# A graph attention edge pass that steps on one TensorE semaphore, with GpSimd's gathers behind it

## The chip, the cores and the metric

One core of a Trainium2 chip. The metric is the device time of one execution in microseconds, from the chip's own counters; the profile is a separate execution of the same program, traced instruction by instruction. A time of before is the median of three runs.

## What is computed

One block over 6250 nodes with 256 channels and 200000 edges sorted by their destination. The part that the change touches is the attention over edges:

```python
h = (x @ W.T).reshape(n, H, D)            # H = 8 heads of D = 32
h_src, h_dst = h[src], h[dst]
enc = jax.nn.relu(edge_attr @ edge_W.T + edge_b).reshape(-1, H, D)
alpha = (jnp.einsum('ehd,hd->eh', h_src, a_src) + jnp.einsum('ehd,hd->eh', h_dst, a_dst)
         + jnp.sum(enc * h_dst, axis=-1))
alpha = jnp.where(alpha >= 0, alpha, 0.2 * alpha)
amax = jax.ops.segment_max(alpha, dst, num_segments=n)
ex = jnp.exp(alpha - amax[dst])
denom = jax.ops.segment_sum(ex, dst, num_segments=n)
out = jax.ops.segment_sum(h_src * (ex / denom[dst])[..., None], dst, num_segments=n)
```

Around it stand a layer norm, a linear attention layer with its feed forward part, and a feed forward part with eight experts of which each node takes one. The change leaves those alone.

## The kernel before

The kernel runs its stages one after the other: node features and linear attention first, then the edge pass, then routing and experts. The edge pass works through 440 items (`ITEMS`). An item is 512 edges (`SE`) against one tile of 125 nodes. Four items (`G`) make a group, and there are 110 groups (`NG`). The code of every engine is written out for every step `k`, so the order on an engine is the order of the program text, and each engine works on several items at different lags in one step.

For item `n`, in order:

- GpSimd `gather(n)` (L506 to L515): four indirect DMAs, each bringing 128 rows of `h_tab` (272 floats a row) into one of 16 slots (`RING`). It waits for the item's earlier transfers, for `msg_ready` (the message of item n-16 is made, so the slot is free) and for `m_used`.
- ScalarE `load_item` (L735 to L738) brings destinations and edge attributes, three DMAs, into one of four buffers.
- TensorE `e_enc` (L1031) encodes the attributes in two matmuls, ScalarE `e_relu` (L753) takes them through the relu, VectorE `e_onehot` (L1452) compares the destinations with the tile's nodes, TensorE `e_dst` (L1041) spreads the nodes' features in six matmuls.
- VectorE `e_prod` (L1461) multiplies, in two halves, and TensorE `e_sum` (L1062, 16 small matmuls; L1065 on every fourth item) sums by head into bank 7.
- For each group a chain on VectorE, TensorE and ScalarE finds the running maxima across edges and the exponentials: `g_x`, `g_leaky`, `g_fmax` (L1479), `g_smax`, `g_up`, `g_ends`, `g_chain`, `g_fin`, `g_down`, `g_carry`, `g_fmax2` (L1510), `g_smax2` (L1514 and L1515, which signals `x_dif`), `g_exp`, `g_turn`, `g_keep`, `g_delta`, `g_fac`, `g_scale` (L1533).
- ScalarE `keep_asrc` (L760) copies eight columns of the gathered rows one step after the item's encoding, so it waits for the gather; `m_dt` and `m_oneh` (L764 to L775) make another one-hot matrix.
- VectorE `m_msg` (L1541) weights the gathered rows, TensorE `m_sum` (L1100, 8 matmul instructions in the trace) sums them by node, VectorE `m_acc` (L1550) adds the sum to the accumulator.

`LM` is the lag of `m_msg` behind the item's first step: 11 before.

SyncE runs a loop over groups (L440 to L445): `load_idx(g)` waits until the items of group g-2 are gathered and issues four DMAs (L412), then `load_links(g-2)` waits for `x_dif` of the group two before that one and issues 24 small DMAs (16 at L420 into `pen`, 8 at L423 into `link`). `g_fmax` of a group waits for all 24 (`links_in`).

Before, each kind of TensorE work signals a semaphore of its own: `enc_mm`, `d_ready`, `r_ready`, `ends_up`, `ends_down`, `ex_turned`, `m_used`. ScalarE, VectorE and GpSimd wait for these one by one. In the bank 7 code, what TensorE writes and the others read shares one bank, which `bank7_read` guards.

Of the kernel before, what the change touches and what calls it, by code (L numbers as in the profile page):

```python
# [20 lines left out]
ALU = mybir.AluOpType  # L21
ACT = mybir.ActivationFunctionType
X = mybir.AxisListType.X
ds = bass.ds
# [3 lines left out]
P = 125  # L28
# [5 lines left out]
SE = 512  # L34
# [15 lines left out]
CLEARS = 10  # L50
# [4 lines left out]
LM = 11  # L55
# [51 lines left out]
def build_program(nc, io):  # L107
    stack = ExitStack()
    with stack:
# [42 lines left out]
        def slot(n):  # L152
# [103 lines left out]
        fin = sb("fin", [33, 128], at=mem_e)  # L256
        carry = sb("carry", [128, 2], at=mem_e)
        xs, exr = small[0], small[3]
# [71 lines left out]
        item_in, oneh_t_ready, d_ready, enc_ready = sems("item_in", EB // 2), sem("oneh_t_ready"), sem("d_ready"), sem("enc_ready")  # L330
        enc_mm, prod_ready, r_ready, zeroed = sem("enc_mm"), sem("prod_ready"), sem("r_ready"), sem("zeroed")

        links_in = sems("links_in")
        x_kept, x_local, ends_up, ends_read, links_made, ends_down, carry_read, x_dif, x_exp, ex_turned, ex_kept = (
            sem("x_kept"), sem("x_local"), sem("ends_up"), sem("ends_read"), sem("links_made"), sem("ends_down"), sem("carry_read"), sem("x_dif"), sem("x_exp"), sem("ex_turned"), sem("ex_kept"))
        dl_ready, fac_ready, acc_scaled = sem("dl_ready"), sem("fac_ready"), sem("acc_scaled")
        dt_ready, msg_ready, oneh_ready, dist_ready, acc_added, m_used = sem("dt_ready"), sem("msg_ready"), sem("oneh_ready"), sem("dist_ready"), sem("acc_added"), sem("m_used")
# [47 lines left out]
        def _(sp):  # L385
# [59 lines left out]
            sp.wait_ge(m_used, ITEMS)  # L445
# [28 lines left out]
        def _(pool):  # L474
# [29 lines left out]
            def gather(n):  # L504
# [6 lines left out]
                wait(pool, m_used, n - RING)  # L511
# [21 lines left out]
            clear(fin[:, :], 0.0)  # L533
# [9 lines left out]
            pool.wait_ge(m_used, ITEMS)  # L543
# [48 lines left out]
        def _(act):  # L592
# [142 lines left out]
            def load_item(b, s):  # L735
                act.dma_start(dstb[b][:, :], dst16[ds(s * SE, SE)].partition_broadcast(P)).then_inc(item_in[b // 2], 16)
                for a in range(KC):
                    act.dma_start(att[b][32 * a:32 * a + 24, :], attrx[:, ds(s * SE, SE)]).then_inc(item_in[b // 2], 16)  # L738
# [10 lines left out]
            def e_relu(n):  # L749
                act.wait_ge(enc_mm, n + 1)  # L750
# [5 lines left out]
            def keep_asrc(n):  # L756
                i = n % G
                act.wait_ge(gathered[n % NGS], 64 * (n // NGS) + 64)
                wait(act, r_ready, n - i - G)
# [6 lines left out]
            def m_oneh(n):  # L766
# [7 lines left out]
                wait(act, m_used, n - NM + 1)  # L774
                act.activation(oneh[n % NM][:, :, :], dist[q][:, :, :], ACT.Relu, bias=1.0, scale=-1.0).then_inc(oneh_ready, 1)  # L775

            def g_x(g):
                act.wait_ge(r_ready, G * g + G)
                wait(act, x_dif, g)
                act.activation(xs[:, :], bank[7][:, 0:128], ACT.Copy).then_inc(x_kept, 1)  # L780
# [5 lines left out]
            def g_keep(g):  # L786
                act.wait_ge(ex_turned, g + 1)
# [5 lines left out]
            def g_fac(g):  # L793
                act.wait_ge(ends_down, g + 2)
# [18 lines left out]
            for k in range(ITEMS + LM + 2):  # L813
# [5 lines left out]
                if (g := group_at(k, 5)) is not None:  # L819
                    g_x(g)  # L820
                if (g := group_at(k, 9)) is not None:
                    g_exp(g)
                if (g := group_at(k, 10)) is not None:
                    g_keep(g)
                if 0 < k < ITEMS - EB + 1:
                    b = k % EB
                    act.wait_ge(d_ready, k)
# [4 lines left out]
                if k % G == 0 and 8 <= k < ITEMS + 8:  # L832
                    s_dt, t_dt = item_regs(act, 0, k - 8), item_regs(act, 1, k - 8)
                if 0 <= k - 8 < ITEMS:
# [3 lines left out]
                if (g := group_at(k, 12)) is not None:  # L838
                    g_fac(g)

            act.wait_ge(m_used, ITEMS)
# [44 lines left out]
        def _(pe):  # L886
# [139 lines left out]
            def e_enc(n):  # L1026
                b = n % EB
                pe.wait_ge(item_in[b // 2], 96 * (n // EB) + 96)
# [785 lines left out]
```

## Time and profile before

| what | value |
|---|---|
| median of the runs | 4996.56 us (4992.17 to 4997.22) |
| the profiled execution | 5021.78 us |
| its span, first to last instruction | 5019.9 us |
| granted TensorE clock, mean | 0.864 |
| TensorE matmuls busy | 3767.7 us, 75% |
| VectorE busy | 2605.4 us, 52% |
| ScalarE busy | 2110.6 us, 42% |
| GpSimd busy | 2107.5 us, 42% |
| edge pass, first `m_acc` to last | 984.1 to 4232.6 us, 440 items |

Busy time is what an engine's own instructions took; waiting and DMA issue are not in it. In a group of rows, "idle before" is the time that the engine stood still just before these instructions, and the name behind the arrow is what the trace sees end that wait. "remote" or "another core or an unknown queue" is said where the trace finds nothing that ended at that time.

### The profile page before, as it was taken

Reading aid. Unit: us, or ns where it says so; the run is one execution under the profiler, and the core shown is the slowest. Engines: PE = TensorE matmul, PEld = TensorE weight load, DVE = VectorE, ACT = ScalarE, POOL = GpSimd, SP = SyncE. Lnnn points to the kernel's source line nnn. Section 1 sums busy time; section 2 is a strip of 40 time slices with the busy share of each in tenths; the row PEclk is TensorE's granted clock in tenths of the full one; section 3 lists DMA queues with packets and bytes.
Section 4 is the critical chain, followed back from the end, with each engine's and each line's share of the span. In section 5 each row is a group of like instructions: output and inputs, shape, how many; then the busy total and the mean of one; then the engine's idle time right before and its main releaser. Section 6 shows DMA issues by size and latency. Waiting matters only on the chain.

```text
span 5019.9 us, 89713 instructions
## 1 busy us (share of the span) xinstructions
PE 3767.7 (75%) x22054; PEld 2525.2 (50%) x22055; DVE 2605.4 (52%) x6056; ACT 2110.6 (42%) x5703; POOL 2107.5 (42%) x2172
## 2 busy tenths in 40 slices
PE   4788998477777677677777777777777775972999
PEld 3357887244444444444444444444444443862888
DVE  5557555455555555555555655555655555440121
ACT  3212332244444444454444545444454444442332
POOL 4120000455555555555555555555555551015111
PEclk8889999788888888888888888888888888986999
DMA  4610111344433344343433444334444443002110
GB/s 153 218 60 18 32 33 37 89 100 102 106 99 101 99 104 105 100 105 103 105 104 103 110 105 110 103 102 104 106 111 107 104 110 119 30 22 58 36 37 29
DMA packets 352311, 449.36 MB, mean 90 GB/s; under 512 B 170970, under 2 KB 275163, under 8 KB 350456
## 3 DMA queue, kind: packets, MB, share of 16 engines
q0 software_dynamic: 95568, 267.78, 20.6%
q10 hardware_dynamic: 108050, 122.83, 7.9%
q1 hardware_dynamic: 148231, 53.53, 4.4%
q8 instruction: 174, 2.85, 0.2%
q14 instruction: 288, 2.36, 0.1%
HBM read 389.57 MB, written 55.13 MB: 89 GB/s over the span
## 4 chain that ended last, share of the span: by engine, by line
PE 48%; another core or an unknown queue 16%; issue 13%; DVE 11%; ACT 4%; ACTq 4%; DMA 3%; POOL 1%; DVEq 1%; SPq 0%; POOLq 0%
PE bank L1100 9%; PE bank L1041 8%; PE bank L1184 4%; PE bank L1196 4%; PE bank L1144 4%; PE bank L1006 3%; PE bank L1015 3%; PE bank L1062 3%; DVE prod L1461 3%; PE bank L1031 2%; ACT dist L771 2%; DVE msg L1541 2%; PE bank L919 1%; PE bank L1065 1%
## 5 line engine op out<-in xcount | busy, mean ns | idle before, releaser
L515 POOL DMA_INDIRECT al<-h_tab,idx x976 | 1022.7, 1048 | 794.9 <-issue 298.5
L515 POOL DMA_INDIRECT gbuf<-h_tab,idx x784 | 840.5, 1072 | 808.8 <-issue 383.8
L753 ACT ACTIVATE enc<-bank,eb 128x512 f32<-128x512 f32 x880 | 555.9, 682 | 1468.2 <-remote 1262.5
L1062 PE MATMUL bank<-prod,hsel 128*32 128x128 f32 x7040 | 325.6, 309 | 763.0 <-issue 505.1
L1041 PE MATMUL bank<-oneh_t,hbt 125*128 125x512 bf16 x2640 | 842.3, 463 | 46.8 <-issue 39.4
L1062 PEld LDWEIGHTS bank<-prod,hsel 128*32 128x32 f32 x7040 | 192.1, 119 | 934.3 <-issue 634.2
L1461 DVE SCALAR_TENSOR_TENSOR prod<-enc,adst,bank 128x512 f32<-128x512 f32 x880 | 629.1, 736 | 37.9 <-remote 32.4
L1100 PE MATMUL bank<-msg,oneh 128*125 128x264 f32 x2352 | 628.5, 413 | 26.9 <-DVE r L1550 18.0
L1100 PEld LDWEIGHTS bank<-msg,oneh 128*125 128x125 f32 x2352 | 488.1, 208 | 173.0 <-issue 61.1
L771 ACT ACTIVATE dist<-iota_n,dtile 128x125 f32<-128x125 f32 x1760 | 550.9, 384 | 0.2
L1041 PEld LDWEIGHTS bank<-oneh_t,hbt 125*128 x2640 | 257.5, 111 | 493.0 <-issue 365.6
L1550 DVE TENSOR_TENSOR r<-r,bank 125x264 f32 x440 | 188.2, 428 | 559.4 <-remote 263.5
L1100 PE MATMUL bank<-al,oneh 128*125 128x264 f32 x1168 | 314.0, 413 | 10.9 <-DVE r L1550 7.2
L1100 PEld LDWEIGHTS bank<-al,oneh 128*125 128x125 f32 x1168 | 241.5, 208 | 90.1 <-issue 34.3
L775 ACT ACTIVATE oneh<-dist 128x500 f32<-128x500 f32 x440 | 272.7, 620 | 14.1 <-PE bank L1100 0.2
L1031 PE MATMUL bank<-att,ew_bf 24*128 24x512 bf16 x880 | 206.1, 453 | 48.9 <-DMA att<-attrx 28.3
L524 POOL MEMSET al<- 128x2 f32 (+1 forms) x3 | 0.3, 113 | 535.7 <-DMA accd<-al 535.6
L880 ACT ACTIVATE al<-bank,b1f 128x256 f32<-128x256 f32 x224 | 106.2, 474 | 270.6 <-PE bank L1184 270.6
L1541 DVE TENSOR_TENSOR msg<-al 128x1056 f32<-128x1056 f32 x163 | 203.8, 1250 | 0.1
L1184 PE MATMUL bank<-al 128*128 128x256 f32 x896 | 200.8, 383 | 0.7 <-ACT al L874 0.7
L1015 PE MATMUL bank<-r 128*125 128x256 f32 x800 | 200.2, 379 | 0.0
L1006 PE MATMUL bank<-r 128*128 128x250 f32 x800 | 199.2, 378 | 0.0
(255 smaller groups left out, 5405.9 us busy)
## 6 DMA issues: line engine op xcount, KB each, us to landing
dstb<-dst ACTq DMA_DIRECT2D x440, 125.0 KB
al<-pen_d SPq DMA_DIRECT2D x1760, 4.0 KB
att<-attrx ACTq DMA_DIRECT2D x880, 24.0 KB
al<-h_tab,idx POOLq DMA_INDIRECT x976
link<-links SPq DMA_DIRECT2D x880, 0.2 KB
gbuf<-h_tab,idx POOLq DMA_INDIRECT x784
attrx<-al ACTq DMA_DIRECT2D x8, 1176.0 KB, 12.3
hsplit<-hb POOLq DMA_DIRECT2D x25, 375.0 KB, 5.4
```

What stands on the lines that cost most here:

```text
L515: pool.indirect_dma_start(slot(n)[:, c, :], None, h_tab, bass.IndirectOffsetOnAxis(ap=idx[g % 2][:, k:k + 1], axis=0)).then_inc(gathered[n ...
L753: m = act.activation(enc[n % 2][:, k, :], bank[k][:, :], ACT.Relu, bias=eb[:, k:k + 1])
L771: m = act.activation(dist[q][:, c, :], iota_n[:, :], ACT.Abs, bias=dtile[n % NDT][:, c:c + 1], scale=-1.0)
L1006: m = pe.matmul(bank[FB3[j % 4]][:, 0:W2T], w1m[:, k, j * 128:(j + 1) * 128], ynT[:, k, :], start=(k == 0), stop=(k == KC - 1))
L1015: m = pe.matmul(bank[3 + u][0:P, 0:C], f1[:, j, u * P:(u + 1) * P], w2m[:, j, :], start=(j == 0), stop=(j == JF - 1))
L1031: m = pe.matmul(bank[k][:, :], ew_bf[32 * k:32 * k + 24, k * 128:(k + 1) * 128], att[b][32 * k:32 * k + 24, :], start=True, stop=True)
L1041: m = pe.matmul(bank[2 + 2 * q + k][:, :], hbt[:, ds(t & (HT - 1), 1), a, k * 128:(k + 1) * 128].rearrange("p t c -> p (t c)"), oneh_t[q][ ...
L1062: m = pe.matmul(bank[7][32 * c:32 * c + 32, 0:128], hsel[:, i, :], prod[n % 2][:, k, c * 128:(c + 1) * 128], start=(i == 0 and k == 0), st ...
L1100: m = pe.matmul(bank[6][0:P, 0:HO], oneh[n % NM][:, c, :], msg[n % NM][:, c, :], start=(c == 0), stop=(c == 3))
L1184: m = pe.matmul(bank[FB[j % 4]][:, 0:256], w1f[:, k, j * 128:(j + 1) * 128], xdT[:, k, :], start=(k == 0), stop=(k == KC - 1))
L1461: m = v.scalar_tensor_tensor(prod[q][:, k, :], enc[q][:, k, :], adst[:, k:k + 1], bank[2 + 2 * q + k][:, :], ALU.add, ALU.mult)
L1541: v.tensor_tensor(msg[n % NM][:, :, :].rearrange("p c (h e) -> p c h e", h=H), slot(n)[:, :, 8:HR].rearrange("p c (h e) -> p c h e", h=H), ...
```

## The change

Each TensorE step now ends with one signal, `stepped`, on the last matmul of `e_enc(k + 1)` (in the last steps on `m_sum`). All seven semaphores above are gone. VectorE and ScalarE wait for `stepped` once, at the top of a step, and what a step takes from TensorE is what TensorE finished in the step before. For this the lags grow: `LM` is 14, the group's chain takes lags 6, 9, 11 and 13 instead of 6, 7, 8 and 11 on VectorE, and some buffers are doubled (`fin`, `xs`, `smax2`). TensorE's step now runs spread, message sum, sum by head, the group's small matmuls, next encoding. GpSimd's gather of item n waits for `stepped` to reach n, which is the end of TensorE's step n-2. Each item buffer has a semaphore of its own (`item_in[b]`) instead of one for two. SyncE's loop keeps its text; only its wait after the loop names `stepped`.

```diff
-LM = 11
+LM = 14
+STEPS = ITEMS + LM + 2
@@ GpSimd, gather(n)
                 wait(pool, msg_ready, n - RING + 1)
-                wait(pool, m_used, n - RING)
+                wait(pool, stepped, min(n, STEPS) if n >= RING else 0)
@@ ScalarE
             def e_relu(n):
-                act.wait_ge(enc_mm, n + 1)
                 wait(act, prod_ready, n - 1)
...
-            for k in range(ITEMS + LM + 2):
+            for k in range(STEPS):
+                act.wait_ge(stepped, k + 1)
+                if (g := group_at(k, 6)) is not None:
+                    g_x(g)
...
-                    m_dt(k - 8, s_dt[k % G], t_dt[k % G])
-                if 0 <= k - 10 < ITEMS:
-                    m_oneh(k - 10)
...
+                    m_dt(k - 12, s_dt[k % G], t_dt[k % G])
+                if 0 <= k - 13 < ITEMS:
+                    m_oneh(k - 13)
+                if (g := group_at(k, 11)) is not None:
+                    g_exp(g)
@@ TensorE
+            e_enc(0).then_inc(stepped, 1)
+            for k in range(ITEMS + LM + 1):
                 if k % EB == 0 and k < ITEMS:
                     t = item_regs(pe, 1, k, EB)
+                if k < ITEMS:
+                    e_dst(k, t[k % EB])
+                if 0 <= k - LM - 1 and k + 1 < ITEMS:
+                    m_sum(k - LM - 1)
                 bank7_read(k)
                 if 0 <= k - 2 < ITEMS:
                     e_sum(k - 2)
...
+                if k + 1 < ITEMS:
+                    e_enc(k + 1).then_inc(stepped, 1)
+                else:
+                    m_sum(k - LM - 1).then_inc(stepped, 1)
@@ VectorE
-                g1, g2, g3, g4 = (group_at(k, lag) for lag in (6, 7, 8, LM))
+                g1, g2, g3, g4 = (group_at(k, lag) for lag in (6, 9, 11, 13))
+                v.wait_ge(stepped, k + 1)
```

TensorE, one step in the middle of the edge pass, before (the encoding and the spread of one item, then the message sum; `msg`, `oneh`, `prod` as above, `ident` is the identity):

```order
L1062 MATMUL bank<-prod,hsel 32x128 [waits prod_ready,x_kept]
L1062 MATMUL bank<-prod,hsel 32x128 x7
L1092 MATMUL bank<-ident,al 1x8 [waits x_exp]
L1093 MATMUL bank<-ident,al 128x128
L1031 MATMUL bank<-att,ew_bf 128x512 [waits enc_ready,item_in1]
...
L1037 REGISTER_ALU [waits oneh_t_ready]
...
L1041 REGISTER_ALU [waits prod_ready,node_in]
...
L1041 MATMUL bank<-oneh_t,hbt 128x512
...
L1100 MATMUL bank<-al,oneh 125x264 [waits acc_added,oneh_ready,msg_ready]
```

The same of the changed kernel:

```order
L1035 REGISTER_ALU [waits oneh_t_ready]
...
L1039 REGISTER_ALU [waits prod_ready,node_in]
...
L1039 MATMUL bank<-oneh_t,hbt 128x512
...
L1098 MATMUL bank<-msg,oneh 125x264 [waits acc_added,oneh_ready,msg_ready]
...
L1061 MATMUL bank<-prod,hsel 32x128 [waits prod_ready,x_kept]
L1061 MATMUL bank<-prod,hsel 32x128 x7
L1079 MATMUL bank<-ident,fin 128x2 [waits links_made]
L1085 MATMUL bank<-dl,oneh 125x8 [waits oneh_ready,dl_ready]
L1029 MATMUL bank<-att,ew_bf 128x512 [waits enc_ready,item_in3]
```

The message sum and its wait for the accumulator moved ahead of the sum by head, and the encoding moved to the end, where it carries the step's signal.

VectorE, the step in which a group's first scan (`g_fmax`) stands, before:

```order
L1550 ISA [waits acc_added,m_used]
L1550 TENSOR_TENSOR r<-r,bank 125x264
L1474 SCALAR_TENSOR_TENSOR al<-al 128x128 [waits ex_turned,x_kept]
L1461 SCALAR_TENSOR_TENSOR prod<-enc,adst,bank 128x512 [waits r_ready,enc_ready,d_ready]
L1479 SCALAR_TENSOR_TENSOR al<-al 128x128 [waits own_step,links_in1]
L1461 SCALAR_TENSOR_TENSOR prod<-enc,adst,bank 128x512
L1483 SCALAR_TENSOR_TENSOR al<-al 128x128 [waits own_step]
...
L1452 TENSOR_SCALAR oneh_t<-dstb,nid 125x512
L1541 TENSOR_TENSOR al<-al 128x1056 [waits m_used,gathered5,ex_kept]
```

and of the changed kernel:

```order
L1548 ISA [waits acc_added,stepped]
L1548 TENSOR_TENSOR r<-r,bank 125x264
L1462 SCALAR_TENSOR_TENSOR prod<-enc,adst,bank 128x512 [waits enc_ready]
L1474 SCALAR_TENSOR_TENSOR al<-al 128x128 [waits x_kept]
L1462 SCALAR_TENSOR_TENSOR prod<-enc,adst,bank 128x512
L1479 SCALAR_TENSOR_TENSOR al<-al 128x128 [waits own_step,links_in1]
...
L1455 TENSOR_SCALAR oneh_t<-dstb,nid 125x512
L1483 SCALAR_TENSOR_TENSOR al<-al 128x128 [waits own_step]
L1540 TENSOR_TENSOR al<-gbuf,al 128x1056 [waits gathered2,ex_kept]
```

All waits for TensorE but the first are gone; the scan stands behind both products instead of between them, with the wait for the links still on it.

## Rows read from the trace of the kernel before

**Rows 1.** Windows: busy time of each engine in the middle of the edge pass
```profile
core 0: us, PE busy (x) PEld busy (x) DVE busy (x) ACT busy (x) POOL busy (x), PEclk, DMA share, GB/s
1200.00:4000.00 2800.00, 2057.82 (x13187) 1215.80 (x13187) 1596.52 (x3253) 1352.63 (x3805) 1577.34 (x1485) 0.84 0.40 104
```

**Rows 2.** Windows, of line L1550 (`m_acc`, one an item) alone
```profile
core 0: us, DVE busy (x), PEclk, DMA share, GB/s
1200.00:4000.00 2800.00, 158.71 (x371) 0.84 0.40 104
```

**Rows 3.** Waits, 1500 to 3500 us: who waited for whom, us in total, times, longest
```profile
ACT enc L753 <- remote: 768.0, 151, 9.1
...
DVE r L1550 <- remote: 179.1, 50, 6.1
DVE al L1474 <- remote: 162.2, 25, 8.3
...
DVE carry L1506 <- remote: 105.2, 22, 7.0
```

**Rows 4.** Timeline, 2500 to 2520 us, TensorE's work and who saw it (start, us)
```profile
2501.14 0.39 PE L1031 MATMUL bank<-att,ew_bf 24*128 24x512 bf16 x2
...
2502.77 1.95 PE L1100 MATMUL bank<-msg,oneh 128*125 128x264 f32 x8
...
2506.21 0.69 ACT L753 ACTIVATE enc<-bank,eb 128x512 f32<-128x512 f32 x1 [6.16 <-remote]
...
2507.43 0.43 DVE L1550 TENSOR_TENSOR r<-r,bank 125x264 f32 x1 [3.49 <-remote]
...
2514.17 0.29 DVE L1474 SCALAR_TENSOR_TENSOR al<-al 128x128 f32<-128x128 f32 x1 [6.32 <-remote]
...
2518.25 0.61 PE L1031 MATMUL bank<-att,ew_bf 24*128 24x512 bf16 x2
...
2518.90 0.69 ACT L753 ACTIVATE enc<-bank,eb 128x512 f32<-128x512 f32 x1 [0.65 <-PE bank L1031]
```

**Rows 5.** Timeline of GpSimd, 2491 to 2520 us
```profile
2500.72 0.94 POOL L515 DMA_INDIRECT al<-h_tab,idx  x1 [0.30 <-issue]
...
2505.07 0.95 POOL L515 DMA_INDIRECT al<-h_tab,idx  x1 [0.30 <-issue]
2508.16 0.95 POOL L515 DMA_INDIRECT al<-h_tab,idx  x1 [2.15 <-remote]
...
2511.92 0.95 POOL L515 DMA_INDIRECT al<-h_tab,idx  x1 [0.30 <-issue]
2518.62 0.94 POOL L515 DMA_INDIRECT al<-h_tab,idx  x1 [5.75 <-DVE al L1541]
```

**Rows 6.** Groups by line, 1200 to 4000 us: busy us, mean ns, idle before
```profile
L515 POOL DMA_INDIRECT al<-h_tab,idx x837 | 884.9, 1057 | 688.9 <-issue 256.9 <-DVE msg L1541 177.7 <-PE bank L1100 106.3
L1041 PE MATMUL bank<-oneh_t,hbt 125*128 125x512 bf16 x2232 | 712.2, 463 | 35.1 <-issue 34.4
L515 POOL DMA_INDIRECT gbuf<-h_tab,idx x648 | 693.6, 1070 | 534.0 <-issue 185.4 <-PE bank L1100 119.0 <-DVE msg L1541 103.2
L1461 DVE SCALAR_TENSOR_TENSOR prod<-enc,adst,bank 128x512 f32<-128x512 f32 x744 | 532.0, 736 | 0.3
...
L771 ACT ACTIVATE dist<-iota_n,dtile 128x125 f32<-128x125 f32 x1484 | 464.5, 384 | 0.2
...
L775 ACT ACTIVATE oneh<-dist 128x500 f32<-128x500 f32 x371 | 229.9, 620 | 11.8
```

**Rows 7.** Timeline of TensorE, 4220 to 4240 us: the last steps, without gathers
```profile
4227.69 2.02 PE L1100 MATMUL bank<-msg,oneh 128*125 128x264 f32 x8 [0.50 <-DVE r L1550]
4230.43 2.02 PE L1100 MATMUL bank<-msg,oneh 128*125 128x264 f32 x8 [0.72 <-DVE r L1550]
```

**Rows 8.** Timeline of SyncE: first and last issues of three groups' links
```profile
2593.49 1.73 SPq L420 DMA_DIRECT2D al<-pen_d  x4
...
2608.71 1.21 SPq L423 DMA_DIRECT2D link<-links  x2
...
2528.51 1.38 SPq L420 DMA_DIRECT2D al<-pen_d  x4
...
2545.38 1.17 SPq L423 DMA_DIRECT2D link<-links  x2
...
1373.31 4.37 SPq L420 DMA_DIRECT2D al<-pen_d  x4
...
1393.18 1.21 SPq L423 DMA_DIRECT2D link<-links  x2
```

**Rows 9.** The page's DMA issues: KB each, median us from issue to landing
```profile
hsplit<-hb POOLq DMA_DIRECT2D x25, 375.0 KB, 5.4
```

**Rows 10.** Timeline of VectorE: the scan of the first of these groups, its step
```profile
2630.46 0.43 DVE L1550 TENSOR_TENSOR r<-r,bank 125x264 f32 x1 [4.17 <-PE bank L1100]
...
2631.90 0.42 DVE L1479 TENSOR_TENSOR_SCAN al<-al 128x128 f32<-128x128 f32 x1
...
2633.45 1.25 DVE L1541 TENSOR_TENSOR msg<-al 128x1056 f32<-128x1056 f32 x1
```

**Rows 11.** Timeline of VectorE: the step that signals `x_dif` (L1515)
```profile
1369.89 0.43 DVE L1550 TENSOR_TENSOR r<-r,bank 125x264 f32 x1 [0.18 <-issue]
...
1372.84 0.29 DVE L1515 TENSOR_TENSOR al<-al 128x128 f32<-128x128 f32 x1
```

More of the change, by code:

```diff
@@ L49 @@
 NM = 3
-CLEARS = 10
+CLEARS = 11
 NDT = 4
@@ L255, in build_program @@
         tot = sb("tot", [33, H, 17], at=mem_e)
-        fin = sb("fin", [33, 128], at=mem_e)
+        fin = [sb(f"fin{q}", [33, 128], at=mem_e) for q in range(2)]
         carry = sb("carry", [128, 2], at=mem_e)
-        xs, exr = small[0], small[3]
+        xs, exr = [small[0], al[:, spare + 1280:spare + 1408]], small[3]
+        smax2 = al[:, spare + 1152:spare + 1280]
         fmax, smax = al[:, spare + 128:spare + 256], al[:, spare + 288:spare + 416]
@@ L532, in _ @@
             clear(tot[:, :, 16:17], -BIG)
-            clear(fin[:, :], 0.0)
+            for q in range(2):
+                clear(fin[q][:, :], 0.0)
             clear(edge[:, :, 0:1], -BIG)
@@ L773, in m_oneh @@
                 act.wait_ge(dist_ready, n + 1)
[L774 removed]
                 act.activation(oneh[n % NM][:, :, :], dist[q][:, :, :], ACT.Relu, bias=1.0, scale=-1.0).then_inc(oneh_ready, 1)
             def g_x(g):
[L778 to L780 removed]
+                wait(act, x_dif, g - 1)
+                act.activation(xs[g % 2], bank[7][:, 0:128], ACT.Copy).then_inc(x_kept, 1)
             def g_exp(g):
@@ L1040, in e_dst, with readings @@
                     for a in range(3):
[L1041 to L1042 removed]
+                        pe.matmul(bank[2 + 2 * q + k][:, :], hbt[:, ds(t & (HT - 1), 1), a, k * 128:(k + 1) * 128].rearrange("p t c -> p (t c)"), oneh_t[q][:, :], start=(a == 0), stop=(a == 2))
             def bank7_read(k):
[L1046 to L1047 removed]
+                def readings(lag):
+                    return min((k - lag) // G, NG - 1) + 1 if k >= lag else 0
+                if k % G == 2:
+                    wait(pe, x_kept, readings(6))
                 if k % G == 1:
[L1049 to L1052 removed]
+                    wait(pe, ends_read, readings(9))
+                    wait(pe, ex_kept, readings(13))
                 if k % G == 3:
[L1054 removed]
+                    wait(pe, carry_read, readings(11))
+                    wait(pe, fac_ready, readings(15))
             def e_sum(n):
@@ L1112, in _ @@
                     e_sum(k - 2)
-                elif k % G == 2:
+                elif k % G == 2 and k < ITEMS + LM:
                     new_sums()
@@ L1556, in _ @@
             e_onehot(0, item_regs(v, 1, 0)[0])
-            for k in range(ITEMS + LM + 3):
+            for k in range(STEPS):
                 if k % G == 0:
```

162 lines of the change are left out of this document (69 added, 93 removed).

## The prediction

> **What bounds the kernel now.** The table by windows comes first. In the middle of the edge pass no engine is full: TensorE is busy 2058 of 2800 us, GpSimd 1577, VectorE 1597, ScalarE 1353 [rows 1]. Line L1550 runs once an item, 371 times in 2800 us [rows 2], so a step takes 2800 / 371 = 7.55 us, and 440 of them make about two thirds of the span. What a step is made of must be read from the waits. The largest are put down to nothing that the trace knows: ScalarE waits 768 us for "remote" ahead of the relu, VectorE 179, 162 and 105 us ahead of three places that wait for TensorE [rows 3].
>
> The timeline shows what that is. TensorE's encoding ends at 2501.14 + 0.39 = 2501.53 us, and the relu that waits for it starts at 2506.21, 4.7 us later. The message sum ends at 2504.72, and the add behind it starts at 2507.43, 2.7 us later [rows 4]. TensorE had finished; its signals arrived late. GpSimd's view of the same stretch says when. Its gathers ran from 2500.72 to 2506.02 and from 2508.16 to 2512.87 [rows 5], and the waiters start 1.41 us after the first end (2507.43) and 1.30 us after the second (2514.17) [rows 4]. After a pause of 5.75 us on GpSimd a gather began at 2518.62 [rows 5], and an encoding that ended at 2518.86 was seen at 2518.90, at once [rows 4]. My reading: a TensorE signal that falls into a run of gathers is often held until about 1.3 us after the run's last one, but early in a run that follows a long pause it gets through. Signals of VectorE and ScalarE show nothing of the kind; the large "remote" waits are all for TensorE.
>
> **A step of GpSimd before.** A gather takes (884.9 + 693.6) / 1485 = 1.063 us [rows 6], with 0.30 between the four of an item [rows 5]: 4.25 + 0.90 = 5.15 us an item. All idle time before gathers is 688.9 + 534.0 = 1222.9 us [rows 6], 3.29 an item, of which 0.90 lies inside it; 2.40 us stand between items. 5.15 + 2.40 = 7.55. Of this sum only the 2.40 can move.
>
> **The signals.** Five or so TensorE signals a step become one. The Trainium skill, in "TensorE: Matmul & The Clock Gate", section "The cost: per-tile semaphore tail", prices a signal of a matmul at 26 ns: by that, four fewer would be 0.1 us a step, some 46 us in all. This case's trace shows delays of 2.7 and 4.7 us instead, which no count of signals explains; I take nothing for the count alone.
>
> What matters is where the one signal falls. Call R the moment at which the others see it. VectorE adds the message sum by about R + 0.55 (0.43 us of work, 0.1 to wake). TensorE waits for that, then does the message sum (1.95 us), the sums and the group's small matmuls (about 1.1) and the encoding (0.4 to 0.6) [rows 4]: its next signal is given near R + 4.1, or R + 6 where the granted clock is at its lower level (0.84 on average [rows 1]). The spread, 6 x 463 ns or less [rows 6], lies ahead of R, under the wait. GpSimd starts its gathers about 0.85 us after R: it began at 2508.16, and the add that the same signal let go had begun at 2507.43 [rows 4, 5]. They end at R + 6.0. So the next signal nearly always falls into the second half of the gathers, never in a pause, and arrives 1.3 us after their end: R + 7.3. The idle time between items is then the 2.15 us before the gather at 2508.16 [rows 5], which is just such a case, instead of 2.40. A step of 7.30 us saves 0.25.
>
> Some signals will get through as at 2518.90. Then the next item's gathers follow after 0.30 us rather than 2.15, which saves 1.85, and the signal after that falls late in a double run and is held. The rows show a free one only behind a pause of 5.75 us, which the new order doesn't have; bounds are 0 and all. I take one in ten: 0.2 us. The step is 7.1 us.
>
> **The other engines in 7.1 us.** VectorE's longest step holds the add of 0.43 us, two products of 0.74, the message of 1.25 and some 1.5 to 2 us of the group's chain [rows 4, 6, 10]: 5 to 5.5. ScalarE has two relus of 0.69, four absolute values of 0.38, one relu of 0.62 and its DMA issues [rows 4, 6], about 5.5. Both hide behind the wait for R. `m_msg` of item n-16 is done in the step before GpSimd needs it, so `msg_ready` no longer ends GpSimd's wait (it did for 5.75 us in [rows 5]); the gather lands two steps before ScalarE copies from it, and a step is longer than a gather run, so a late gather costs nothing.
>
> **SyncE, which the change does not edit.** `load_links` of group j waits for `x_dif` of group j-2, now in step 4j + 3 (lag 11) instead of 4j (lag 8); the scan that waits for the links stays in step 4j + 6. Before, the last issue was at 2609.92 and the scan at 2631.90 [rows 8, 10]: 22.0 us to spare. Three steps of 7.55 take 22.6 of them: nothing is left. The issues take 16.4, 18.0 and 21.1 us in the three groups shown [rows 8]; I take 18. Landing has no row for these transfers; it lies between 0 and the 5.4 us of a far larger one [rows 9]; I take 2, nearer the lower end for their size. Round the loop: 18 + 2, then from the scan to the end of its step 2634.70 - 2631.90 = 2.8 [rows 10], then the next step up to `x_dif`, 1373.13 - 1369.89 = 3.2 and 0.6 for the one-hot and wakes that now stand ahead: 3.8 [rows 11]. That is 26.6 us a group, 6.65 a step, under 7.1 by 1.8 us a group. A group with 21.1 us of issues takes 29.7, 7.4 a step. Over the mix I add 0.1: 7.2 us.
>
> **Ends.** `LM` adds three steps. The last ones, without gathers, take 2.74 us each (4230.43 less 4227.69 [rows 7]): 8 us more. Doubled buffers and per-item semaphores cost nothing that waits.
>
> **The sum.** 440 x (7.55 - 7.20) = 154 us less, 8 more: -146 us. The profiled execution took 5021.8 us with a span of 5019.9; the median of the runs is 4996.6. I take the difference off the median: 4850 us.
>
> **Rivals.**
> - *Free signals.* With one signal a step the hold rarely takes. For it: the case at 2518.90. Against it: signals in the second half of a run are those that the rows show held. Gathers alone would allow 5.15 + 0.30 = 5.45 us; the link loop stops it at 6.65: 4996.6 - 396 + 8 = 4610 us.
> - *The link loop decides* (slower). One mechanism: SyncE's 24 issues start three steps later, and the scan waits for them. It decides from the point where issues and landing exceed 30.2 - 6.6 = 23.6 us. With the slow group's 21.1 us everywhere and a landing of 4 it is 31.7 us a group, 7.93 a step: +167 + 8 = 5170 us. For it: nothing is left of the 22 us, and SyncE issues beside gathers. Against: two of three groups shown need 18 or less.
> - *Nothing moves.* The signal is held as long as before and GpSimd's pause stays at 2.40: +8 us, 5005. This is also the case in which the change doesn't do what it says, as where the added wait of GpSimd is satisfied before its other waits are.
>
> **How the numbers follow.** Forecast 0.50, free signals 0.18, link loop 0.20, nothing 0.12. The predicted time is the forecast's. Its own range, from no free signal (4890) to one in five (4760), with the loop's share, is 4760 to 4950. For 8 in 10, the range goes down to 4680, halfway into the first rival, and up to 5080, halfway to the second. A measurement here tells about 0.2% from no change. Faster: the forecast, the first rival and a little of the last, 0.70; within 0.2%: 0.07; slower: 0.23.
>
> **What would show it.** In the profile of the changed kernel: L1548 takes 7.2 us from one to the next; GpSimd's idle time before an item's first gather is near 2.15 us in most items, and its 5.75 us waits for `m_msg` are gone; waits for "remote" end on VectorE, ScalarE and GpSimd at one moment a step, about 1.3 us after a gather run. If the scan L1479 has idle time before it of over a few tenths, the link loop is at work and the second rival gains. If the pauses of GpSimd are mostly 0.30, it is the first. The prediction is wrong altogether if TensorE's signals arrive at once and the step is still over 7 us, for then something other than the hold sets the pace.

## The result and the profile after

| what | before | after |
|---|---|---|
| median of the runs beside each other, us | 4994.36 (4981.86 to 4997.22, 4 runs) | 4745.41 (4742.08 to 4750.28, 4 runs) |
| the profiled execution, us | 5021.78 | 4742.83 |
| its span, us | 5019.9 | 4741.0 |
| edge pass, first `m_acc` to last, us | 984.1 to 4232.6 | 1000.1 to 3953.4 |
| granted TensorE clock, mean | 0.864 | 0.891 |

The ratio is 0.9507 (95% interval 0.9488 to 0.9526): 249 us less. In the profiled executions it is 279 us, since that of before was 27 us over its median. The edge pass became 3248.5 - 2953.3 = 295 us shorter and starts 16 us later, and what follows it is as long as before (4741.0 - 3953.4 = 787.6 us against 787.3). So all of it is the step. The granted clock rose with it; no run holds the clock fixed, so what share of the step it gave is open.

The table by windows, of the same 2800 us as [rows 1] (of which the last 47 lie behind the edge pass), and of `m_acc` alone in the 2700 us from 1200 to 3900:

```profile
1200.00:4000.00 2800.00, 2194.11 (x14244) 1276.69 (x14248) 1679.63 (x3541) 1463.23 (x4151) 1762.42 (x1580) 0.88 0.46 115
```
```profile
1200.00:3900.00 2700.00, 168.61 (x394) 0.89 0.46 115
```

394 items in 2700 us are 6.85 us a step, where [rows 2] gave 7.55. Every engine has a larger share than in [rows 1], and none is full.

The groups by line of the changed kernel, 1200 to 3900 us (columns as in [rows 6]), show GpSimd's side:

```profile
L517 POOL DMA_INDIRECT al<-h_tab,idx x875 | 964.8, 1103 | 500.9 <-issue 240.9 <-remote 181.9 <-PE bank L1029 57.1
L517 POOL DMA_INDIRECT gbuf<-h_tab,idx x700 | 794.5, 1135 | 442.0 <-issue 184.7 <-remote 177.4 <-PE bank L1029 61.2
L1039 PE MATMUL bank<-oneh_t,hbt 125*128 125x512 bf16 x2364 | 654.2, 417 | 220.5 <-issue 132.0 <-DVE oneh_t L1455 84.7 <-DMA hbt<-hsplit 3.7
```

The busy time is 1759.3 / 1575 = 1.117 us a gather (1.063 before), the idle time 942.9 / 1575 x 4 = 2.39 us an item (3.29 before). Less the 0.90 inside an item, 1.49 us stand between items by this sum, and 1.41 when each pause is measured by itself. Of the waits for `m_msg` that [rows 6] shows on GpSimd, 11 are left in this stretch (39.6 us), and "remote" and the encoding's signal (L1029) stand in their place.

The sum over a group hides the shape. Worked out item by item over the same stretch of each trace (a pause under 0.5 us counts as one of 0.30):

| kernel | run of four gathers, us | pause between items, mean us | pauses of 0.30 | pauses over 3 us |
|---|---|---|---|---|
| before | 5.23 | 2.32 | 138 of 358 | 109 |
| after | 5.45 | 1.41 | 112 of 394 | 6 |

The long pauses are what went. The timeline of GpSimd in the changed kernel (start us, us, idle before in brackets), and behind it the encoding that carries the step's signal (L1029) and VectorE's add that waits for it (L1548):

```profile
2453.88 0.95 POOL L517 DMA_INDIRECT gbuf<-h_tab,idx  x1 [0.30 <-issue]
2456.73 0.94 POOL L517 DMA_INDIRECT gbuf<-h_tab,idx  x1 [1.90 <-remote]
2457.97 1.44 POOL L517 DMA_INDIRECT gbuf<-h_tab,idx  x1 [0.30 <-issue]
2459.72 1.78 POOL L517 DMA_INDIRECT gbuf<-h_tab,idx  x1 [0.30 <-issue]
2461.81 1.00 POOL L517 DMA_INDIRECT gbuf<-h_tab,idx  x1 [0.30 <-issue]
2463.12 0.94 POOL L517 DMA_INDIRECT al<-h_tab,idx  x1 [0.30 <-issue]
...
2466.87 1.41 POOL L517 DMA_INDIRECT al<-h_tab,idx  x1 [0.30 <-issue]
2470.06 0.94 POOL L517 DMA_INDIRECT al<-h_tab,idx  x1 [1.78 <-remote]
```
```profile
2453.12 0.39 PE L1029 MATMUL bank<-att,ew_bf 24*128 24x512 bf16 x2
2455.99 0.43 DVE L1548 TENSOR_TENSOR r<-r,bank 125x264 f32 x1 [3.23 <-remote]
...
2459.51 0.39 PE L1029 MATMUL bank<-att,ew_bf 24*128 24x512 bf16 x2
2460.70 0.43 DVE L1548 TENSOR_TENSOR r<-r,bank 125x264 f32 x1
...
2464.36 0.37 PE L1029 MATMUL bank<-att,ew_bf 24*128 24x512 bf16 x1
2469.30 0.43 DVE L1548 TENSOR_TENSOR r<-r,bank 125x264 f32 x1 [1.84 <-remote]
```

Two kinds of step stand here. The signal of 2453.51 is seen at 2455.99, 1.16 us after the run of gathers ended (2454.83), and GpSimd goes on at 2456.73. The signal of 2459.90 falls into a gather that takes 1.78 us instead of 0.95, and is seen by 2460.70, in the middle of the run; the next item's gathers then follow after 0.30 us. The signal of 2464.73, given in that double run, is held to 2469.30.

The page's groups show what waits on SyncE, which was not so before (VectorE's scan of [rows 10] had no idle time before it):

```profile
L1479 DVE TENSOR_TENSOR_SCAN al<-al 128x128 f32<-128x128 f32 x110 | 46.7, 425 | 317.5 <-DMA link<-links 257.3
```

And the timeline of one group, SyncE's issues and the scan that waits for them:

```profile
2473.62 1.53 SPq L422 DMA_DIRECT2D al<-pen_d  x4
...
2488.24 1.33 SPq L425 DMA_DIRECT2D link<-links  x2
```
```profile
2493.15 0.42 DVE L1479 TENSOR_TENSOR_SCAN al<-al 128x128 f32<-128x128 f32 x1 [3.08 <-DMA link<-links]
```

The last issue ends at 2489.57, and the scan starts 3.6 us later, where [rows 8, 10] had 22.0 us. This is no exception. Over 1200 to 3900 us, 95 of the 99 scans of the changed kernel have idle time before them, 2.9 us in the mean:

```profile
L1479 DVE TENSOR_TENSOR_SCAN al<-al x99: 403/425/453, 1208.6 to 3894.9; 128x128 f32<-128x128 f32 x99
its engine sat idle before it (us, times) until:
  DMA link<-links: 234.7, 74
  issue: 56.9, 21
```

The link loop is closed in nearly every group. From `x_dif` to the first issue it takes 1.1 us in the mean, the issues take 16.6, from the last issue to the scan it is 3.2, and from the scan to the next `x_dif` 6.5, in which a wait for the step's signal lies: 27.4 us a group, and four steps of 6.86 are the same 27.4.

### The profile page after: what moved, and what is told of

Same layout as the page of the kernel before. It is cut to its first block, busy times and chain, and to the rows that moved or that the text cites. A ratio compares the mean times of both kernels' runs of the same rounds, so it can differ in the third digit from the quotient of the medians.

```text
span 4741.0 us, 87548 instructions
## 1 busy us (share of the span) xinstructions
PE 3726.2 (79%) x22054; PEld 2471.1 (52%) x22055; DVE 2541.6 (54%) x6056; ACT 2100.9 (44%) x5703; POOL 2200.3 (46%) x2173
## 3 DMA queue, kind: packets, MB, share of 16 engines
q14 instruction: 273, 2.23, 0.1%
## 4 chain that ended last, share of the span: by engine, by line
PE 32%; issue 17%; SPq 15%; DVE 12%; DMA 10%; POOL 6%; another core or an unknown queue 6%; ACT 1%; ACTq 1%; DVEq 0%; POOLq 0%
SPq L422 8%; SPq L425 5%; PE bank L1098 4%; PE bank L1188 4%; PE bank L1200 4%; PE bank L1148 4%; PE bank L1004 4%; PE bank L1013 3%; DMA link<-links 3%; POOL gbuf L517 3%; DMA al<-h_tab,idx 2%; POOL al L517 2%; DVE msg L1540 2%; DVE prod L1462 2%
## 5 line engine op out<-in xcount | busy, mean ns | idle before, releaser
L517 POOL DMA_INDIRECT al<-h_tab,idx x976 | 1069.8, 1096 | 556.3 <-issue 271.3
L517 POOL DMA_INDIRECT gbuf<-h_tab,idx x784 | 887.0, 1131 | 681.0 <-issue 364.5
L1039 PE MATMUL bank<-oneh_t,hbt 125*128 125x512 bf16 x2640 | 738.4, 420 | 255.1 <-issue 143.1
L1098 PE MATMUL bank<-msg,oneh 128*125 128x264 f32 x2352 | 700.4, 449 | 243.1 <-DVE r L1548 217.0
L1039 PEld LDWEIGHTS bank<-oneh_t,hbt 125*128 x2640 | 245.7, 103 | 607.4 <-issue 435.4
L1548 DVE TENSOR_TENSOR r<-r,bank 125x264 f32 x440 | 188.3, 428 | 546.8 <-remote 449.4
L1098 PE MATMUL bank<-al,oneh 128*125 128x264 f32 x1168 | 358.9, 458 | 127.9 <-DVE r L1548 119.9
L1061 PE MATMUL bank<-prod,hsel 128*32 128x128 f32 x7040 | 300.2, 291 | 16.3 <-ACT al L779 12.5
L1061 PEld LDWEIGHTS bank<-prod,hsel 128*32 128x32 f32 x7040 | 174.7, 114 | 195.8 <-issue 180.6
L1029 PE MATMUL bank<-att,ew_bf 24*128 24x512 bf16 x880 | 195.7, 389 | 37.8 <-DMA att<-attrx 27.2
L1479 DVE TENSOR_TENSOR_SCAN al<-al 128x128 f32<-128x128 f32 x110 | 46.7, 425 | 317.5 <-DMA link<-links 257.3
L1533 DVE TENSOR_TENSOR r<-r,fac 125x264 f32 x110 | 47.7, 434 | 300.1 <-PE bank L1029 195.5
```

What stands on the lines that cost most here:

```text
L517: pool.indirect_dma_start(slot(n)[:, c, :], None, h_tab, bass.IndirectOffsetOnAxis(ap=idx[g % 2][:, k:k + 1], axis=0)).then_inc(gathered[n ...
L1039: pe.matmul(bank[2 + 2 * q + k][:, :], hbt[:, ds(t & (HT - 1), 1), a, k * 128:(k + 1) * 128].rearrange("p t c -> p (t c)"), oneh_t[q][:, : ...
L1061: pe.matmul(bank[7][32 * c:32 * c + 32, 0:128], hsel[:, i, :], prod[n % 2][:, k, c * 128:(c + 1) * 128], start=(i == 0 and k == 0), stop=F ...
L1098: m = pe.matmul(bank[6][0:P, 0:HO], oneh[n % NM][:, c, :], msg[n % NM][:, c, :], start=(c == 0), stop=(c == 3))
```

## The experiments

Each ran beside the kernel before on the same chip, and the ratio is to that. The kernel before took 4944.6, 5005.0 and 4943.9 us (medians) on the first three chips used. The kernels `a_no_wait`, `a_signals`, `a_links3` and `b_late_gather` ran on the first of them; `a_again`, `a_links3_three` and the two without gathers on the second; `a_early`, `b_links3` and `b_late_links3` on the third.

### The change again

> The changed kernel itself, on the same chip as the next three, so that they have it beside them. Near 0.951 of before.

4744.15 us, ratio 0.9466 (0.9433 to 0.95). The time is that of the result to within 1.3 us, and so is the step in its trace (6.86 us). Which chip gave the result is not known, so this need not be a second one.

### GpSimd's wait: taken away, loosened, and put alone into the kernel before

```diff
@@ a_no_wait, in gather(n) of the changed kernel
-                wait(pool, stepped, min(n, STEPS) if n >= RING else 0)
@@ a_early, in gather(n) of the changed kernel
-                wait(pool, stepped, min(n, STEPS) if n >= RING else 0)
+                wait(pool, stepped, n - 2 if n >= RING else 0)
@@ b_late_gather, in gather(n) of the kernel before
                 wait(pool, m_used, n - RING)
+                wait(pool, enc_mm, n - 1 if n >= RING else 0)
```

> The changed kernel without GpSimd's new wait: a gather waits for the message of item n-16 and no longer for the step signal. The message ends about 5 us into a step, so a run of gathers then starts there and reaches some 3.5 us into the next step. If the wait's place is what brings the gain (the run starts right behind a signal), the time goes back by 100 us or more, to 4850 us and over. If the gain comes from the one signal and the longer lags alone, it stays within 20 us of 4745. If a run that starts late in a step leaves the signal, given at about 4.5 us, in a pause, it gets faster, down to the link loop's floor of some 6.7 us a step, about 4700 us.

5226.63 us, ratio 1.0606 (1.0524 to 1.0689).

> The changed kernel, with GpSimd's wait for stepped two steps looser (n-2 in place of n), all else the same. If the wait helps because it ties each run of gathers to one TensorE signal, then a looser wait lets GpSimd run two items ahead when it can, double runs come back in part, and the time lies between the changed kernel's (4745) and that without the wait (ratio 1.06): ratio 0.97 to 1.05. If the phase alone counts, which is the same with n-2 once GpSimd has caught up, it stays at 0.945 to 0.955. GpSimd's other wait, for the message 16 items back, allows it to be about one step ahead of where the present wait puts it, so the former is likelier.

5241.33 us, ratio 1.0579 (1.0526 to 1.0632).

> The kernel before with one wait more: GpSimd's gather of item n also waits for enc_mm to reach n-1, the encoding of step n-2. This is the change's second half alone, with five signals a step and the old lags. If the gathers' place is the gain, it is faster than before by 50 us or more. If the old lags need each signal within the step, runs of gathers that start right behind an encoding hold the spread's and the sums' signals every step: slower than before, by 50 to 400 us.

4730.27 us, ratio 0.9592 (0.9518 to 0.9665).

One line, put alone into the kernel before, brings most of the gain. All the rest of the change without that line is 6% slower than before. (That kernel has also lost the wait for `m_used`, which the change took out; no run puts it back, so the 6% is not split between the two.) Two steps looser, the wait does nothing at all, where 0.97 to 1.05 was expected. What happens without it shows in the timeline of GpSimd and of `m_acc` (L1547) in the kernel without the wait:

```profile
2512.00 0.94 POOL L516 DMA_INDIRECT al<-h_tab,idx  x1 [6.93 <-issue]
...
2515.75 1.38 POOL L516 DMA_INDIRECT al<-h_tab,idx  x1 [0.31 <-issue]
2517.43 0.95 POOL L516 DMA_INDIRECT gbuf<-h_tab,idx  x1 [0.30 <-issue]
...
2521.19 0.95 POOL L516 DMA_INDIRECT gbuf<-h_tab,idx  x1 [0.30 <-issue]
2528.54 0.95 POOL L516 DMA_INDIRECT gbuf<-h_tab,idx  x1 [6.40 <-issue]
```
```profile
2516.38 0.37 PE L1028 MATMUL bank<-att,ew_bf 24*128 24x512 bf16 x1
2523.57 0.43 DVE L1547 TENSOR_TENSOR r<-r,bank 125x264 f32 x1 [7.26 <-remote]
2524.14 3.73 PE L1097 MATMUL bank<-msg,oneh 128*125 128x264 f32 x8 [5.99 <-DVE r L1547]
```

Eight gathers, two items, go in one run from 2512.00 to 2522.14. The step's signal is given at 2516.75 and seen at 2523.57, 1.43 us after the end of the double run and 6.8 us late. GpSimd stands for 6.4 us until 2528.54. It waits for a slot, since TensorE, VectorE and the message behind them have two items to make up first: of the items 60 to 399, 85% start their gathers within 1.2 us of the end of the message 16 items back, against 5% in the changed kernel. This repeats; pauses over 3 us are 134 of 340 without the wait, 139 of 338 with the loose one, against 6 of 394. The waits between 1500 and 3500 us, without the wait, then with it:

```profile
DVE r L1547 <- remote: 683.4, 100, 11.9
```
```profile
DVE r L1548 <- remote: 310.7, 126, 6.2
```

### The number of signals

The changed kernel with three more TensorE signals a step that nothing waits for: behind the spread, the sum by head and the message sum.

```diff
+                m.then_inc(more[0], 1)
...
+                m.then_inc(more[1], 1)
...
-                    m_sum(k - LM - 1)
+                    m_sum(k - LM - 1).then_inc(more[2], 1)
```

> The changed kernel with three more signals a step from TensorE (last matmul of the spread, of the sum by head, of the message sum) on semaphores that nobody waits for. If the number of signals is what cost time before, this gives back a large part of the 249 us. If only their place against the gathers counts, the extra ones are held in the same line and let go together with the step's own: within 40 us of 4745, at most 0.1 us a step.

4719.59 us, ratio 0.9562 (0.9488 to 0.9635), step 6.79 us. In microseconds that is 26 less than the changed kernel took in its other runs. By ratio it is 0.6% to 1% more (0.9507 and 0.9466), that is 27 to 47 us on this chip, and its interval holds the first of the two and not the second. The changed kernel was not timed on this chip, so a cost of up to some 50 us is not excluded. Even that is well under the 249 us, and so much the run decides: the number of signals is not what brought most of the gain.

### The links

Three buffers for `pen` and `link`, and SyncE issues a group's links one group earlier; in the changed kernel, in the kernel before, and in the kernel before with the late gather. The edit of the waits and the loop (the third buffer itself is left out here):

```diff
-                wait(sp, x_dif, g - 1)
+                wait(sp, x_dif, g - 2)
...
-                load_links(g - 2)
+                load_links(g - 1)
...
```

> The changed kernel with three buffers for pen and link instead of two, and SyncE's links of a group issued one group earlier. The wait of the scan L1479 for the links (257 us by the page of the changed kernel) must go. If the link loop sets part of the pace, the time falls by 60 to 200 us (step 6.86 to between 6.4 and 6.7 us). If the hold of the signals sets it alone, the wait moves to the step's start and the time stays within 20 us of 4745.

4669.2 us (4664.87 to 4678.12), ratio 0.9468 (0.9395 to 0.9541). The scan has no idle time before it any more, the step is 6.68 us.

> The kernel before, with three buffers for pen and link and the links' DMAs issued a group earlier, nothing else. If the link loop holds only the changed kernel (in the kernel before the last issue lies 22 us ahead of the scan), this moves the time by less than 0.3%, step 7.55 us. If SyncE's issues cost the kernel before something in another way (for instance beside gathers), up to 1.5% are gained as in the changed kernel, where the same edit took 75 us off.

4935.04 us, ratio 0.9976 (0.9942 to 1.001): nothing, as the 22 us to spare say.

> The kernel before with GpSimd's wait for the encoding of item n-2 (b_late_gather) and the three link buffers: every TensorE signal of its own, the old lags, no merged signal. Theory: the wait fixes where the signals fall in the gathers and the link loop is the only other thing between the two, so it comes to the time of the changed kernel with three link buffers, ratio to the kernel before 0.945 to 0.955. If b_late_gather was not held by the links (its scan still has slack of some 10 us), the three buffers give nothing and it stays at 0.955 to 0.962; then the longer lags or the merged signal are worth the last per cent. Rival: the merged signal is needed for the gain beyond 4%, the ratio stays at 0.96.

4734.17 us, ratio 0.9563 (0.9516 to 0.9611). Nothing over the late gather alone (4730.27): with the old lags the links are in time. The 0.945 to 0.955 of the theory was missed; it is the other case that was named.

The four corners together: on the old order the late gather gives 4730 us with two or three buffers. The new order gives 4745 with two and 4669 with three. So the new order with its single signal is worth some 65 us (4734 against 4669, with the kernel before at 4944 on both chips), but the three steps by which it starts the links later take about as much back: 76 us by the times (4745 against 4669, different chips), 50 beside the run with extra signals on the same chip. How much it is stays rough: the ratios, 0.9466 on one chip and 0.9468 on another, show next to nothing between the two kernels (11 us if 0.9466 held on this chip too). The step in the traces, 6.86 against 6.68 us, and the idle time before the scan, 291.6 us against none, are on the side of the times. The pauses of 0.30 us fit: 173 of 393 in the new order with three buffers, 100 of 393 in the old with the late gather. Of the kernels that do the whole work this one is the fastest on these three chips.

### The gathers taken away

From item 16 on, GpSimd issues no gather and only counts; the rows that the messages weight are those of the first items, so that part of the computation is left out. Done to the changed kernel and to the kernel before.

```diff
-                for c in range(4):
+                if n >= RING:
+                    pool.sem_inc(passed, 1)
+                for c in range(4 if n < RING else 0):
```

> The changed kernel without the gathers of items 16 to 439: GpSimd waits as before and counts up a semaphore instead, and the slots keep the rows of the first 16 items (that part of the computation is left out). If gathers hold TensorE's signals, every stepped arrives within 0.1 us of its matmul's end in the middle of the edge pass, no wait for remote is left there, and a step takes what VectorE, ScalarE or the link loop need, 5.3 to 6.3 us: 4200 to 4500 us. If the delay is TensorE's own, the delays stay and the time stays over 4650 us.

4098.74 us (2 runs), ratio 0.818 (0.8142 to 0.8218): under the 4200 to 4500 that were expected.

> The kernel before with the same gathers left out. If the hold by gathers is all that the change works on, the five signals a step arrive at once here too, and the old order is as fast as the new one without gathers or faster: within 100 us of the changed kernel without gathers. If the one signal is worth something by itself, this one is over 100 us slower than that.

4238.48 us (2 runs), ratio 0.8459 (0.841 to 0.8508). It is 140 us slower than the changed kernel without gathers, on the same chip: of the two cases that were named, the one in which the new order is worth something by itself. So where no signal is held, the one signal with its longer lags still gives 0.3 us a step. Which of its parts gives it, no run shows.

VectorE's wait for `m_acc` (L1561) in the changed kernel without gathers, 1200 to 3900 us, has no "remote" left in it:

```profile
L1561 DVE TENSOR_TENSOR r<-r,bank x402: 417/429/431, 1203.5 to 3307.2; 125x264 f32 x134
...
  PE bank L1042: 110.1, 204
  PE bank L1111: 11.0, 9
```

By the trace's records, at most 1% of the step's signals come over 0.3 us after their matmul, against 95% in the changed kernel (mean 2.23 us). 402 items in 2104 us are 5.25 us a step. What TensorE, VectorE, ScalarE and SyncE need together is thus 5.25; the gathers bring it to 6.86. With the gathers went their transfers as well (45 GB/s over the stretch against 115), so this run does not tell whether GpSimd's issuing or the transfers hold the signals.

### Three gathers instead of four

The kernel with three link buffers, and three gathers an item from item 16 on; the rows of the fourth column are left out.

```diff
-                for c in range(4):
+                for c in range(4 if n < RING else 3):
```

> The changed kernel with three link buffers, and with three gathers an item instead of four from item 16 on (the fourth column's rows are left out, an older item's stand there). A run of gathers gets 1.25 us shorter. If a step is the start of the run, the run, and the hold behind it, it takes 1.0 to 1.4 us less a step than the same kernel with four: 440 to 600 us less than that kernel. If other engines set the pace, under 0.4 us less a step.

4159.95 us (4154.58 to 4165.64), ratio 0.8301 (0.827 to 0.8332): 509 us less than with four (on another chip), which is 509 / 424 = 1.20 us an item. The gather with its 0.30 us measured 1.13 + 0.30 = 1.43. The run of gathers and the tail behind it set most of the step: 1.20 of the 1.43 us came off it. At 5.48 us it is close to the 5.25 of the other engines.

### A pause inside the run, and a chip that is different

Ahead of the fourth gather of every item GpSimd clears a small tile five times; the rest as with three link buffers.

```diff
                 for c in range(4):
                     k = 4 * (n % G) + c
+                    if c == 3 and n >= RING:
+                        for _ in range(5):
+                            pool.memset(idle[:, :], 0.0).then_inc(paused, 1)
+                            pauses[0] += 1
+                            pool.wait_ge(paused, pauses[0])
```

> The changed kernel with three link buffers (a_links3: step 6.68 us), and ahead of the fourth gather of every item GpSimd clears a small tile five times, each waiting for the last, about 1.3 us in which it issues no gather. Theory: a held TensorE signal is let go once GpSimd issues no gather for somewhat over 1 us, whether at the end of a run or inside it. The step's signal is given from 4.1 to 6 us after the last was seen, that is about the third and fourth gather, so those given before or in the pause are let go in it and the next item's gathers follow after 0.30 us: the run grows by 1.3 us and the idle time between items shrinks from 1.17 to 0.3 to 0.6, step 6.9 to 7.3 us, ratio to the kernel before 0.96 to 0.985. Rival: only the end of an item's four gathers lets a signal go, or only a long gather; then the idle time stays at 1.2 to 2.1 and the step is 7.9 us or more, ratio 1.02 to 1.05.

4664.61 us (4657.26 to 4673.7), ratio 1.112 (1.1067 to 1.1173). The time was about that without the pause on another chip, but the ratio says something else: on this fourth chip the kernel before took 4195.59 us (4171.52 to 4210.3, seven runs), 750 to 810 us less than on the other three.

The timeline of this kernel, GpSimd (the first four lines), then the encoding (L1038) and the add that waits for it (L1557):

```profile
2471.93 0.94 POOL L526 DMA_INDIRECT gbuf<-h_tab,idx  x1 [0.30 <-issue]
2473.18 0.94 POOL L526 DMA_INDIRECT gbuf<-h_tab,idx  x1 [0.30 <-issue]
...
2477.23 0.95 POOL L526 DMA_INDIRECT gbuf<-h_tab,idx  x1 [0.27 <-POOL idle L523]
2478.48 1.93 POOL L526 DMA_INDIRECT gbuf<-h_tab,idx  x1 [0.30 <-issue]
```
```profile
2472.88 0.39 PE L1038 MATMUL bank<-att,ew_bf 24*128 24x512 bf16 x2 [1.81 <-ACT enc L764]
2473.42 0.43 DVE L1557 TENSOR_TENSOR r<-r,bank 125x264 f32 x1 [2.77 <-PE bank L1038]
2479.32 0.39 PE L1038 MATMUL bank<-att,ew_bf 24*128 24x512 bf16 x2
2479.86 0.43 DVE L1557 TENSOR_TENSOR r<-r,bank 125x264 f32 x1 [0.20 <-PE bank L1038]
```

The signal of 2473.27 falls into the gather of 2473.18 to 2474.12 and is seen at 2473.42, at once. That of 2479.71 falls into the gather from 2478.48, and is seen at 2479.86. Of 274 signals given inside a gather here, none came over 0.24 us late. In the changed kernel on its own chip, 99% of 338 came over 0.3 us late (median 2.31). With the pause, GpSimd never waits: run 6.49 us, then 0.30, 387 times of 387, a step of 6.80.

So the run can't tell the two theories about the pause apart, since nothing was held for it to let go. It shows something that no theory here had: on this chip the hold seems not to be there. The pause alone doesn't explain it, because signals given in gathers far from a pause arrive at once as well, and because the kernel before, which has no pause, is 15 to 16% faster there, and with all its gathers faster than without them on the second chip (4195.59 against 4238.48). Nor were there fewer transfers: 116 GB/s from 1200 to 3800 us. As an estimate, with the 1771 us that the rest takes in the trace of before, its edge pass took 2424 us there, 5.51 a step. That is its run of 5.23 and a pause of 0.30, but it is also what it takes without gathers on the second chip (2452 us, 5.57 a step), so which of the two sets the pace there is open. But the kernel before and the changed kernel were not traced on that chip, and the changed kernel was not timed on it. What the change is worth there stays open. An estimate from the rows: a GpSimd that never waits needs 5.2 to 5.45 us of run and 0.30 a step in either order, so by that I would expect little between the two. Against it stand the 140 us between the orders without gathers.

## Why the prediction was right, point by point

- **What bounds the kernel** held on the chips on which the change was timed. TensorE's signals are held while GpSimd issues gathers. Taking the gathers away took away the lateness (95% to 1%) and 1.6 us of the step. What holds them, the issuing or the transfers behind it, no run separates. That it was read as a property of the kernel was too wide: one of four chips seems not to have it, and the trace of one chip can't show that.
- **The place of the signal.** It was put at R + 4.1 to R + 6, into the second half of the run; 338 of 394 signals lay inside a gather. The release was put 1.3 us after the run's end. The trace has a mean of 0.96, the middle half between 0.6 and 1.2, and a normal pause is 1.85 us and not 2.15: 0.3 us a step too much.
- **Free signals.** Taken as one in ten, from a rule that they need a long pause ahead. They were 112 of 394, 28%, and by another way: a held signal gets through in mid-run, and 92 of 101 that did came during a gather that took 1.3 us or more instead of 0.95 (72 of 112 in the kernel with three link buffers). Which of the two is the cause, the trace does not say. 0.28 x 1.55 = 0.43 us where 0.2 was taken. With both, the pause is 0.72 x 1.85 + 0.28 x 0.30 = 1.42 us (1.41 measured) instead of 1.95.
- **The run itself** was taken over from before, 5.15 us. Item by item it was 5.23 there, since not every gap inside is 0.30, and it is 5.45 now, the gathers being 1.117 us instead of 1.063. Why they are longer is open: more transfers (115 GB/s against 104) do not explain it alone, since the late gather in the kernel before moves 115 as well and has 1.076. This took 0.3 us of the above back. The prediction left the term out.
- **The link loop.** "Nothing is left" of the 22 us, which is so, and +0.1 us a step. The prediction had the loop at 26.6 us a group, under the step in most groups. It is 27.4 and closed in nearly every one: landing 2.5 us for the 2 taken, issues 16.6 for the 18, and 6.5 + 1.1 us for the 6.6, in which the hold has its part. Taking the wait away gave 50 to 76 us by the times, 0.11 to 0.17 a step, and less by the ratios.
- **The sum.** 5.45 + 1.41 = 6.86 us against 7.20, which is 0.34 x 440 = 150 us. The measured gain is only 103 us more than forecast, since the step of 7.55 came from an execution 25 us above the median, the edge pass starts 16 us later where 8 were taken for the ends, and it got 295 us shorter where 440 x 0.69 would be 304. The step that was mis-sized is the pause, by its two parts; they have one sign and come to 0.54 us a step, of which the longer run hid 0.30 (and the 0.1 for the links is in the measured pause). The forecast's own range in the prediction mixes two countings: the 4890 for no free signal leaves the links' 0.1 out (with it, 7.40 a step, it is 4938), and the 4760 has it. Nothing rests on that.
- **Number of signals.** Nothing was taken for it. By "TensorE: Matmul & The Clock Gate", section "The cost: per-tile semaphore tail", of the Trainium skill, at 26 ns a signal, three more a step would have cost an estimated 34 us; the run with them is 26 us below the changed kernel by its time and 27 to 47 above it by the ratio, so no run here shows whether the estimate holds. Either is well under the 249 us.
- **What the wait does** was not in the prediction as a term of its own. It said where gathers would start, and not what they would do without the wait. The runs show that it is the change: alone it gives 0.9592, and without it the rest gives 1.0606. By the code, the slot of item n-16 comes free with the message in VectorE's step n-2 (n-5 before). GpSimd without the wait starts right behind that message, inside the step, so its run covers the step's signal and holds it, and the next message comes late in turn. With the wait it starts behind the signal. Nearly the same gain came with the seven old semaphores (the step with the late gather is 6.86 us too), so that five signals became one is not what brought it. What the new order gives by itself shows only where the links (65 us) or the gathers (140 us) are out of the way.
- **The rivals.** Free signals went halfway. The link loop is at work by the prediction's own sign, 2.9 us of idle time before the scan where "a few tenths" would do, but it closes at 6.86 us a step and not at 7.93, and without it the step is still 6.68. "Nothing moves" fell.

## What to carry to other kernels

If one engine's work delays another's signals, tie its start to one such signal, at a place at which the next falls due as its run ends: a prefetch that starts ahead of the signal holds it, and then waits itself for what the signal would have let go. Long runs alone are not the harm. Of the 220 runs between pauses in the kernel with three link buffers, 39 have three items or more, and it is the fastest; in the kernel without the wait it is 31 of 182. What the fast one lacks is pauses over 3 us (0 of 393 against 134 of 340). Before a loop is given longer lags, count the spare time of each queue that the change doesn't touch. And time such a kernel on more than one chip before it is tuned around a delay.

## What was not expected of the hardware

- A TensorE signal given while GpSimd issues indirect DMAs came 2.31 us late in the median (up to 5.32 in the changed kernel), released about 1 us after the run's last gather (mean 0.96), or in mid-run, mostly during a gather of 1.3 us and more (92 of 101 here). No signal of VectorE or ScalarE that has a record came over 0.02 us late, but the records of over 40% of them are missing in this trace. For VectorE the waits say the same: all 91 message sums for which TensorE waited and whose add ended inside a gather started 0.15 us after it, as did the 144 others.
- On one chip of the four on which the experiments ran this was absent: 274 such signals, none over 0.24 us late, and the kernel before in 4195.59 us instead of 4944 to 5005.
- The mean granted clock was 0.891 in the changed kernel and 0.864 before, and the spread's matmul went from 463 ns [rows 6] to 417.
